# Moving the key half of a rotation, a block transpose, two copies and four transfers inside a fused audio block

## The reference, cut to what matters

```python
h = tok(x)                      # 16 tokens -> 8 per group, attention among the 8, added to the query
h = h + attn(layernorm(h))      # 128 rows per block: 12 query heads, 3 key/value heads of 64, rotary, softmax
h = h + ffn(layernorm(h))       # 192 -> 768, gelu, 768 -> 192

# attn, shortened
q, k, v = x @ Wq, x @ Wk, x @ Wv          # 768, 192, 192 columns
q, k = apply_rope(q), apply_rope(k)       # [x1*c + x2*s, -x1*s + x2*c]
attn = softmax(q @ k.T * SCALE)
out = (attn @ v) @ Wo
```

## Time and profile before

| engine | busy us | share of span |
|---|---|---|
| TensorE matmul (PE) | 1005.1 | 89% |
| TensorE weight load (PEld) | 867.8 | 77% |
| VectorE (DVE) | 829.2 | 73% |
| ScalarE (ACT) | 728.2 | 64% |
| GpSimd (POOL) | 437.4 | 39% |
| the 16 DMA engines | | 37.8% of their time |

### The profile page before, as it was taken

One profiled execution on the slowest core, in us unless ns is written; L12 is line 12 of the kernel. 1 busy time (PEld: TensorE's weight loads), 2 busy tenths in 40 slices (PEclk: granted clock), 3 DMA queues, 4 the chain that ended last, 5 costly groups with the idle time before them and its releaser, 6 DMA issues. The chain is left out here.

```text
span 1130.0 us, 24498 instructions
## 1 busy us (share of the span) xinstructions
PE 1005.1 (89%) x7232; PEld 867.8 (77%) x7232; DVE 829.2 (73%) x2095; ACT 728.2 (64%) x2530; POOL 437.4 (39%) x583
## 2 busy tenths in 40 slices
PE   3788999999999999999999999999999999999876
PEld 2567878787877888787778878788878778887865
DVE  2677777777777787787778778777778777878751
ACT  2455666677676677667667766666766766776651
POOL 0333434443444343343444344434334343433430
PEclk7798999999999999999999999999999999999999
DMA  5233434333433433343443344344334334333331
GB/s 162 66 97 101 128 106 121 121 109 101 134 114 106 130 115 103 118 128 109 118 121 109 110 127 122 100 130 122 102 108 132 109 114 126 112 110 118 109 105 38
DMA packets 139936, 127.49 MB, mean 113 GB/s; under 512 B 30993, under 2 KB 123025, under 8 KB 139921
## 3 DMA queue, kind: packets, MB, share of 16 engines
q1 hardware_dynamic: 137632, 124.16, 37.0%
q10 hardware_dynamic: 2288, 3.15, 0.8%
HBM read 70.63 MB, written 56.62 MB: 113 GB/s over the span
## 5 line engine op out<-in xcount | busy, mean ns | idle before, releaser
L300 ACT ACTIVATE E<-ring,m_neg 128x128 f32<-128x128 f32 x768 | 271.3, 388 | 75.2 <-DVE m_neg L511 75.1
L400 POOL TENSOR_TENSOR E<-E,e_rcp 128x512 f32<-128x512 f32 x192 | 198.4, 1040 | 289.4 <-DVE e_rcp L531 286.3
L511 DVE TENSOR_REDUCE m_neg<-ring 128x4 f32<-128x512 f32 x192 | 122.6, 681 | 103.9 <-PE ring L707 103.9
L392 POOL TENSOR_TENSOR q_tok<-rot_c,rot_s 128x384 f32<-128x384 f32 x128 | 126.5, 999 | 149.2 <-DVE rot_s L489 149.2
L300 ACT ACTIVATION_READ_ACCUMULATOR E<-ring,m_neg 128x1 f32 x768 | 174.2, 227 | 0.0
L707 PEld LDWEIGHTS ring<-qkT 64*128 64x128 f32 x1536 | 93.0, 192 | 77.1 <-ACT qkT L294 76.6
L707 PE MATMUL ring<-qkT 64*128 64x128 f32 x1536 | 105.4, 285 | 52.0 <-ACT qkT L294 52.0
L522 DVE STREAM_TRANSPOSE EB<-E 128x512 f32<-128x512 f32 x192 | 134.3, 700 | 17.7 <-POOL E L400 17.7
L831 PE MATMUL ring<-wo_sb,OT 128*128 128x192 f32 x768 | 141.8, 336 | 0.7 <-ACT OT L308 0.7
L694 PE MATMUL bank<-wout_sb,G 128*128 128x192 f32 x768 | 135.4, 326 | 2.9 <-ACT G L366 2.9
L831 PEld LDWEIGHTS ring<-wo_sb,OT 128*128 128x128 f32 x768 | 126.4, 194 | 2.8 <-issue 2.2
(11 more groups left out here) (122 smaller groups left out, 2413.3 us busy)
## 6 DMA issues: line engine op xcount, KB each, us to landing
spill<-EB SPq DMA_DIRECT2D x64, 512.0 KB, 2.6
ET<-spill SPq DMA_DIRECT2D x256, 128.0 KB, 2.7
spill<-EB SPq DMA_DIRECT2D x64, 256.0 KB, 2.8
ET<-spill SPq DMA_DIRECT2D x256, 64.0 KB, 2.0
x_sb<-in_x_dram SPq DMA_DIRECT2D x64, 192.0 KB, 2.5
out_dram<-out_sb SPq DMA_DIRECT2D x64, 96.0 KB, 2.3
x_sb<-in_x_dram SPq DMA_DIRECT2D x64, 64.0 KB, 2.4
w_raw<-in_w_att_dram ACTq DMA_DIRECT2D x2, 576.0 KB, 5.1
```

The source lines that it names most:

```text
L300: last = nc.scalar.activation(E[:, a, s * P:(s + 1) * P], RING[a][:, s * P:(s + 1) * P], ACT.Exp, bias=m_neg[:, a, s:s + 1], accum_out=e_s ...
L392: nc.gpsimd.tensor_tensor(q_tok[:, a, c], rot_c[:, a, c], rot_s[:, a, c], ALU.add).then_inc(q_out, 1)
L400: nc.gpsimd.tensor_tensor(e, e, r, ALU.mult).then_inc(prob_out, 1)
L511: nc.vector.tensor_reduce(m_neg[:, a, REP * g:REP * (g + 1)], RING[a][:, 512 * g:512 * (g + 1)].rearrange("p (h k) -> p h k", k=P), AX_X, ...
```

## The change

TensorE's `qk_turned` takes a range of tiles; for a = 1 it is called for the six query tiles before `tok_h` and for the two key tiles after it. ScalarE's `qk_turned(1)` stands before the copy of bank 7 into HH. VectorE rotates query banks 0 and 1 of a = 1 in one go and puts `blocks_turned(0, 2)` after them, before the key bank. SP writes both pieces to DRAM first and then reads both back.

```diff
@@ SP, blocks_moved
                     sp.wait_ge(blocks_out, 6 * q + 3 * a + 2 + k)
                     need(sp, filled[k], 64 * (2 * (q - 1) + a + 1))
                     sp.dma_start(spill[a, :, c], EB[:, a, c]).then_inc(spilled[k], 16)
+                for k, (s0, heads) in enumerate(PIECES):
+                    c = slice(s0 * P, (s0 + heads) * P)
                     need(sp, pv_mm, 4 * (q - 1) + 2 * a + k + 1)
                     sp.wait_ge(spilled[k], 16 * (2 * q + a + 1))
                     for j in range(NB):
@@ ScalarE, step
+                if att:
+                    qk_turned(1)
                 if ffn:
                     act.wait_ge(hT_mm, p)
                     nc.scalar.copy(HH[:].rearrange("p c a t -> p (c a t)"), B7[:]).then_inc(HH_out, 1)
                 if att:
-                    qk_turned(1)
                     for g in range(NKV):
                         score_exp(1, g)
@@ VectorE, step
                 if att:
-                    rotate(1, (0,))
+                    rotate(1, (0, 1))
                     blocks_turned(0, 2, p)
-                    rotate(1, (1, 2))
+                    rotate(1, (2,))
                     keys_added(1)
@@ TensorE, qk_turned and step
-                def qk_turned(a):
-                    for t in range(8):
+                def qk_turned(a, tiles=range(8)):
+                    for t in tiles:
...
                 if att:
-                    qk_turned(1)
+                    qk_turned(1, range(6))
                 if tok:
                     tok_h()
+                if att:
+                    qk_turned(1, (6, 7))
                 if ffn:
                     hn_turned()
```

## The result

The changed kernel takes 1050.7 us (median of 4 runs, 1049.7 to 1053.7) against 1128.6 for the kernel before beside it: a ratio of 0.931, 95% interval 0.930 to 0.932. The forecast was 1058; 77.9 us went instead of 70.5. In a second set, beside the experiments sp_alone, without_pe and split_second, it took 1052.3 against 1131.0 (0.930, 0.929 to 0.931).

The account below looks back on a forecast made before the run. TensorE's own work, busy 30.80 of 33.30 us a step, plus its idle gaps bounds the kernel. 31 steps at 2.16 (67.0), 0.5 in step 0 and 3.0 at the end total 70.5, giving 1058 us; range 1046 to 1080.

Parts of the forecast that it names:

- TensorE's two gaps: TensorE's idle 0.73 us before the second query tiles and 1.65 before the scores; closing them shortens each step.
- ScalarE's order: ScalarE copies queries and keys before bank 7; with the other edits, scores start at 523.37 instead of 525.53.
- a copy that nobody needs so early: ScalarE's 0.58 us copy of bank 7, ahead of the query and key copies; moving it costs nothing under the scores.
- The block transpose behind bank 1: On VectorE, moving it behind query bank 1 costs nothing; GpSimd's second addition ends 0.51 us earlier.
- The keys came 0.31 earlier: VectorE's key additions, ending at 521.98 instead of 522.29 as GpSimd finishes sooner; bounds 0 and 0.6 us.
- tok_h between queries and keys: On TensorE, fills the wait before the keys (521.6 to 522.0); keys come 0.3 us later, leaving no gap.
- The SP order: Writing both pieces before reading adds nothing inside the loop, keeps 0 to 0.3 us a step, saves 3.0 at the end.
- would just miss: With the old SP order, piece two lands at 529.5 while its half of probs_v comes up at 529.4.
- The fear that reads suffer behind a write: Rival 4: piece one's reads, queued behind piece two's write, land late for probs_v; 1136 us, chance 0.03.
- XL next, with 0.3 of slack: Tightest feed: XL ends 534.25, TensorE takes it 534.56; in rival 1, 0.3 us a step lost there; 1070 us, chance 0.24.
- The end term of 3.0: Second half of probs_v in step 32 waits 3.39 us; reading piece two right behind piece one takes 3.0 us off.
- The forecast's own band: Total between 1050 and 1066 us, the forecast with all its parts, given a chance of 0.60.

Follow-up runs that it names:

- sp_alone: The kernel before with only the SP queue's new order (both pieces written, then read): 1122.0 us, ratio 0.993 to the kernel before.
- without_pe: The changed kernel with TensorE's order put back (key tiles ahead of tok_h): 1056.5 us, ratio 0.934 to the kernel before.
- split_second: The changed kernel with token transposes inside the second ffn_second and tok_h between the second sequence's query tiles: 1047.3 us, ratio 0.926 to the kernel before.
- without_sp: The changed kernel with the SP queue's order put back (write and read piece one, then piece two): 1057.8 us, ratio 0.937 to the kernel before.
- before_again: The kernel before, unaltered, run once more for its first steps: one execution, 1131.6 us.
- after_again: The changed kernel, unaltered, run once more: 1052.3 us, ratio 0.930 to the kernel before.

## Why the prediction was right

- **TensorE's two gaps set the step.** Shown. TensorE's busy time did not change (30.80, 30.73), the step shrank by 2.28 us, and the closed gaps are 0.54 (from 0.73 to 0.19), 1.65 and 0.1.
- **ScalarE's order is the main part.** Right, and shown both ways: 1.72 a step alone, 1.51 when only it is missing. The prediction did not price it by itself; its words "a copy that nobody needs so early" hold: HH was ready at 490.02 (489.43 + 0.59), a microsecond before TensorE came to ffn_first at 491.06. VectorE alone stood for it, 0.17 us, at no cost: its first maximum began 1.21 after the scores, as before.
- **The block transpose behind bank 1 is free and brings 0.51.** Right: 0.55 a step when missing. The keys came 0.31 earlier by the lengths taken (0.58 and 0.28); it was 0.40, since GpSimd's copy took 0.50 and not 0.57 and the first addition 0.48 and not 0.58. The first addition ends 0.14 after GpSimd's copy, at 487.96 against 487.82, as the two of the earlier trace rows did.
- **tok_h between queries and keys.** Right in kind, 0.13 to 0.15 a step.
- **The SP order adds nothing in the loop.** Right for the wrong margin. The estimate that the old order "would just miss" inside the shorter step did not come true: without_sp has a step of 31.00. In a step of without_sp the second half of probs_v began 1.98 us after the issue of the last read had ended and found it there; the 2.15, taken in the same way, was one landing near the end, where TensorE did wait. The fear that reads suffer behind a write was empty too: the median landing of the 128 KB reads went from 2.7 to 2.8 us.
- **XL next, with 0.3 of slack.** It kept 0.31.
- **The size: 77.9, not 70.5.** The step was too small in the sum: 2.28 and not 2.16, which is 31 x 0.12 = 3.7 us. In the clock of the step before the change the scores start at 523.24 instead of 523.37: the second query tiles came 0.03 earlier, tok_h 0.07 earlier behind them, and the key tiles took 0.38 us rather than the 0.44 of a pair that begins after a wait. The other 3.7 lie outside the loop, and mostly at the start. By the profiled executions, with before_again and after_again in brackets (a step is counted from its `tok_qk`):

| stretch | in the sum | measured |
|---|---|---|
| first instruction to step 2 | 0.5 + 2.16 = 2.7 | 6.3 (5.1) |
| the 28 steps from there to step 30 | 60.5 | 64.0 (64.9) |
| step 30 to the end | 2 x 2.16 + 3.0 = 7.3 | 7.9 (8.8) |

At the start the sum held nothing for a wait for ET and nothing for the clock. The first execution of the kernel before had both, before_again only the low stretch: its step 1 shrank from 33.88 to 29.42 us, 4.5 where the sum had 2.16, and 2.35 of that is what the low stretch cost. The end term of 3.0 counted one wait for ET, and was less far off. The clock at the end is a matter of the execution: in the kernel before, the output projection behind the 3.39 us wait of the earlier trace rows ran for 3.77 us, in part at the lower clock (0.60 over 4 us there, which the slices of the page are too coarse to show), and the same 12 matmuls take 2.20 after the change; but the changed kernel has its own low stretch of over 3 us further on, from 1038, and after_again has none there.

The forecast's own band (1050 to 1066), given 0.60, holds the median by 0.7 us only, and one of the four executions (1049.7) lies below it. The mechanism was right step by step; that the total stayed inside the band, with the start left unpriced, was partly luck.

## What to carry to other kernels

When one engine is busy for over nine tenths of a loop, list its gaps with their releasers, and for each ask what the releasing engine did first and who needed that; here one copy put ahead of another gave 1.72 us of 2.28. A wait total of a page should be split by place before any of it is left out of a sum: the waits for one tensor outside the loop came to 7.9 us, and the sum here had looked at one of them. What lies in the first steps should be seen in more than one execution before it is priced: the largest of these waits there, 2.16 us, was in one of two executions of the kernel before. An edit on an engine that is not the bottleneck can pay through a third: a transpose moved on VectorE let GpSimd finish earlier, and that gave VectorE one of its own additions back at half its length.

## What the runs showed of the hardware

- A VectorE addition of two SBUF tiles (128 x 128) takes 0.28 us alone. Beside a GpSimd instruction that had begun before it, it ended 0.14 to 0.16 us after that one's end, before and after the change alike, and lasted 0.48 to 0.59 in the steps shown. The Trainium skill, SBUF — State Buffer, section Who interferes with whom, says that a VectorE instruction with two SBUF inputs contends with a GpSimd instruction that reads SBUF, and that the ports they share are an exclusive lock; the trace agrees.
- A stream transpose and the rotation out of PSUM kept their lengths (0.70 and 0.54) wherever GpSimd's additions lay.
- A write ahead of the reads hardly mattered: with two writes (512 and 256 KB) ahead of eight reads on one queue, the median read landed 2.8 us (128 KB) and 2.3 us (64 KB) after its issue, 2.7 and 2.0 before.
- Two idle times of TensorE under 1 us (0.83 and 0.91) before the query tiles were followed by 3 to 7 us at half the clock in five executions of six that had them in step 1; with 0.83 and 0.41, or 0.83 and 0.54, in none of six. The loop's steps before the change have gaps of 0.73 and 1.65 and never lost the clock.
